# Later layers of a graph network: raw rows in places of their own that ScalarE frees, and more places for one-hots, cast halves and rows

## The chip, the cores and the metric

One Trainium2 chip; the program runs on one of its cores. The metric is the time of one execution on the device in microseconds (us), as the median of several runs. Engines are named TensorE (PE in the rows), VectorE (DVE), ScalarE (ACT), GpSimd (POOL) and SyncE (SP).

## The reference

x is 6250 nodes by 256 features; `src` and `dst` are the ends of 100000 edges, sorted by `dst`. Cut to what matters:

```python
xn = _layernorm(x)
h = xn
for layer in range(6):                        # _L0_gnn_ref
    agg = segment_sum(h[src], dst, num_segments=n)
    z = h + agg
    z = z @ W1[layer] + b1[layer]
    z = relu(_batchnorm(z, g1[layer], be1[layer]))
    z = z @ W2[layer] + b2[layer]
    z = _batchnorm(z, g2[layer], be2[layer])
    h = z if layer == 5 else relu(z)
x = x + h + _L0_mix_ref(xn)                   # attention-like mixing by heads of 32
x = x + _L0_ffn_ref(_layernorm(x))            # 8 experts, three 256x256 maps each
```

`_batchnorm` takes mean and variance over all nodes, so each of its twelve calls is a point at which everything waits for the last column.

## The kernel before, in words

The nodes are padded to 49 tiles of 128 (NT), in 7 chunks of 7 tiles (CT, NC). `Zt` holds the features transposed, two blocks of 128 (FB) by all nodes, in SBUF. The edges are 784 tiles of 128 in 7 sections (S) of 112. Of each section 62 tiles (AT) are summed densely: layer 0 builds a matrix of edge counts (`adjacency`, u8, in HBM), and a later layer multiplies it. The other 50 tiles (GS) are gathered row by row. A later layer has these parts:

- **Passage.** ScalarE applies the affine map and relu to a chunk, TensorE transposes it into banks 0 to 3 (`rows_of_h`), VectorE copies the rows into one of three row buffers `Rb` (`copy_rows`, L1543), and SyncE's queue stores them to `y_table` in HBM (`store_rows`, L575). Chunk c uses buffer c % 3, so a copy waits for the store of chunk c - 3. Then 8 warm-up matmuls (`warm`, L905).
- **Dense sums.** For a chunk's rows ScalarE writes the high terms (fp32r) into `Ych` (`high_terms`, L1274), VectorE the low terms, row minus high (`low_terms`, L1550). SyncE loads blocks of the adjacency into three `Land` places; ScalarE casts a block in two halves of 4 and 3 tiles (`cast_half`, L1300) into one of three places `Ac`, waiting for the half three back. TensorE multiplies a half (`dense_half`, L1021: 16 or 12 matmuls of 512 columns); after a block VectorE adds two banks into `Zt` (`add_dense`, L1682), and TensorE's block k waits for the adds of block k - 2. There are 98 halves: 6 come before the first quad, the others are spread over the first 74 quads by `halves_at`.
- **Quads.** 91 quads of up to 4 gathered tiles (N1). GpSimd issues an indirect DMA for each tile (`gather`, L755). The raw rows land in the low-term half of one of four quad places `Gsp` (RQ = 4), two in `G` and two in `BIG`, so the gather of quad n waits for the matmuls of quad n - 4. ScalarE writes the high terms (`quad_high`, L1282), then copies the raw rows to banks 6 and 7 (L1286), because the low terms overwrite them; VectorE writes the low terms from the banks (`quad_low`, L1558). VectorE makes a one-hot matrix for each tile (`one_hots`, L1568) in one of two places, for quad n + 1 as soon as quad n - 1 is done. TensorE multiplies (`quad`, L926); its last matmul signals `s_mmq`, which is also the signal for the dense halves of that step. Each group of three or four quads is summed over high and low terms (`group_rows`, L1655), transposed (L934) and added to `Zt` (`add_group`, L1668).
- **First map.** From quad 75 on (W1G) TensorE does parts of `z @ W1` between quads (`w1_part`, L1050), ScalarE evicts them (L1309), VectorE takes statistics (`z1_stats`: `part_stats`, L1686; `bank_stats`, L1692). Then `bn_coefficients` (aggregation at L1788), ScalarE's affine, and the second map (`w2_stage`, L1104) with statistics in the same manner.

The order on each engine is the order in which the functions write the steps: at step n VectorE does `quad_low(n)`, `one_hots(n + 1)`, the sum of a group that ended, the adds of the halves of step n - 1, the columns of a group, then statistics of step n - 2. Nothing is reordered on the chip, and a wait holds everything behind it on its engine. Layer 0 has GpSimd gather in another way (`raw0`) and takes its quads whole, in fp32; the part after layer 5 (mixing and experts) is not touched.

## Time and profile before

| | us |
|---|---|
| median of the 3 runs shown | 5272.77 |
| lowest, highest | 5271.77, 5281.3 |
| the profiled execution, its own time | 5229.82 |
| its span, first to last instruction | 5228.0 |
| layers 1 to 5, one each (end of the second map to end of the next) | 615.3 to 622.8 |
| the part after layer 5, from 4157 on | 1071 |

Busy times are those of the profiled execution, and an engine's busy time is no sign that it is the limit: what a place costs is read from what ends the idle time there. Start times in a timeline are us from the span's start. "issue" as a releaser means that the profile shows nothing that the engine waited for; "remote" means that the releaser is not among the instructions that were recorded.

### The profile page before, as it was taken

Reading aid. Unit: us, or ns where it says so; the run is one execution under the profiler, and the core shown is the slowest. Engines: PE = TensorE matmul, PEld = TensorE weight load, DVE = VectorE, ACT = ScalarE, POOL = GpSimd, SP = SyncE. Lnnn points to the kernel's source line nnn. Section 1 sums busy time; section 2 is a strip of 40 time slices with the busy share of each in tenths; the row PEclk is TensorE's granted clock in tenths of the full one; section 3 lists DMA queues with packets and bytes.
Section 4 is the critical chain, followed back from the end, with each engine's and each line's share of the span. In section 5 each row is a group of like instructions: output and inputs, shape, how many; then the busy total and the mean of one; then the engine's idle time right before and its main releaser. Section 6 shows DMA issues by size and latency. Waiting matters only on the chain.

```text
span 5228.0 us, 69828 instructions
## 1 busy us (share of the span) xinstructions
PE 4635.8 (89%) x19111; PEld 3326.3 (64%) x19111; DVE 3077.3 (59%) x7552; ACT 3090.9 (59%) x4248; POOL 2980.1 (57%) x3415
## 2 busy tenths in 40 slices
PE   4777899989887899888997998888898899999999
PEld 3555578667764677557775677646776576666665
DVE  6666666455555565545555455555555556666666
ACT  4555533367665676557675667656675435555555
POOL 5565566136662566626665266634666227877776
PEclk8999999999999999999998999989999989999999
DMA  6334454044432554334442354425443410000000
GB/s 208 109 123 130 132 165 144 27 158 152 143 117 68 160 155 145 102 105 145 151 137 85 119 154 152 128 57 166 149 146 114 150 37 8 8 8 8 8 8 8
DMA packets 197182, 560.41 MB, mean 107 GB/s; under 512 B 44306, under 2 KB 63228, under 8 KB 196668
## 3 DMA queue, kind: packets, MB, share of 16 engines
q0 software_dynamic: 109728, 299.78, 20.3%
q1 hardware_dynamic: 79676, 227.39, 12.2%
q10 hardware_dynamic: 7392, 28.90, 1.4%
q8 instruction: 144, 2.36, 0.2%
q14 instruction: 242, 1.98, 0.1%
HBM read 481.66 MB, written 74.24 MB: 106 GB/s over the span
## 4 chain that ended last, share of the span: by engine, by line
PE 54%; DVE 11%; another core or an unknown queue 11%; ACT 10%; issue 9%; POOL 3%; DMA 1%; DVEq 1%; ACTq 0%; POOLq 0%; SPq 0%
PE bank L1021 17%; PE bank L1204 10%; PE bank L1213 6%; PE bank L1104 5%; PE bank L926 4%; PE bank L923 3%; PE bank L969 3%; ACT bank L1286 3%; PE bank L1050 3%; ACT Gsp L1282 2%; ACT Ac L1300 2%; DVE Gsp L1558 2%; DVE onehot L1568 2%; DVE Z L1682 2%
## 5 line engine op out<-in xcount | busy, mean ns | idle before, releaser
L755 POOL DMA_INDIRECT G<-y_table,idx x1416 | 1376.6, 972 | 1335.4 <-DMA y_table<-BIG 512.2
L1021 PE MATMUL bank<-Ac,Ych 128*128 128x512 f32 x7644 | 1909.1, 402 | 166.7 <-issue 86.4
L1021 PEld LDWEIGHTS bank<-Ac,Ych 128*128 128x128 f32 x7644 | 1471.4, 194 | 544.7 <-issue 143.8
L1300 ACT CAST Ac<-BIG 128x2048 fp32r<-128x2048 uint8 (+1 forms) x546 | 916.4, 1688 | 735.7 <-remote 520.2
L755 POOL DMA_INDIRECT BIG<-y_table,idx x870 | 829.1, 953 | 492.2 <-issue 249.5
L1568 DVE TENSOR_SCALAR onehot<-iota,rel 128x128 fp32r<-128x128 f32 x2290 | 513.0, 298 | 696.0 <-remote 550.1
L1558 DVE TENSOR_TENSOR Gsp<-bank,Gsp 128x512 fp32r<-128x512 f32 x875 | 564.1, 685 | 362.6 <-ACT bank L1286 246.1
L2047 DVE TENSOR_TENSOR G<-G,bank 128x448 f32<-128x448 f32 x784 | 462.0, 619 | 215.4 <-ACT G L1464 114.2
L926 PE MATMUL bank<-Gsp,onehot 128*128 128x512 f32 x1750 | 518.7, 414 | 69.9 <-issue 34.2
L1682 DVE TENSOR_TENSOR Z<-Z,bank 128x512 f32 x546 | 373.8, 685 | 207.3 <-PE bank L1021 85.1
L1469 ACT ACTIVATE G<-G,fsh,fsc 128x448 f32<-128x448 f32 x448 | 333.9, 757 | 250.7 <-DVE G L2047 245.1
L1365 ACT CAST BIG<-bank 128x384 f32 (+2 forms) x672 | 276.8, 514 | 269.4 <-PE bank L969 148.1
L926 PEld LDWEIGHTS bank<-Gsp,onehot 128*128 128x128 f32 x1750 | 320.3, 190 | 172.3 <-issue 118.6
L969 PE MATMUL bank<-BIG 128*128 128x408 bf16 (+1 forms) x1302 | 292.6, 348 | 116.4 <-DVE BIG L1580 63.6
L1213 PE MATMUL bank<-BIG,G 128*128 128x256 f32 x1568 | 347.7, 379 | 2.3 <-ACT G L1469 2.3
L1050 PE MATMUL bank<-Z,W 128*128 128x448 f32 (+1 forms) x720 | 310.0, 582 | 39.7 <-ACT Z L1309 29.1
L1213 PEld LDWEIGHTS bank<-BIG,G 128*128 128x128 f32 x1568 | 297.8, 190 | 61.1 <-issue 20.4
L1686 DVE BATCH_NORM_STATS2 bst<-Z 128x6 f32<-128x448 f32 (+1 forms) x324 | 183.4, 608 | 184.9 <-ACT Z L1325 164.4
L923 PE MATMUL bank<-G,onehot 128*128 128x256 f32 x1072 | 276.8, 404 | 6.8 <-DMA G<-y_table,idx 4.1
L1286 ACT COPY bank<-G 128x512 f32<-128x512 f32 x440 | 243.3, 583 | 33.1 <-DVE Gsp L1558 31.7
L1104 PE MATMUL bank<-Z,W 128*128 128x448 f32 x672 | 254.2, 540 | 5.9 <-ACT Z L1256 5.9
L1050 PEld LDWEIGHTS bank<-Z,W 128*128 128x128 f32 x720 | 150.4, 217 | 168.2 <-issue 155.4
(229 smaller groups left out, 5785.5 us busy)
## 6 DMA issues: line engine op xcount, KB each, us to landing
BIG<-adjacency SPq DMA_DIRECT2D x273, 448.0 KB
BIG<-y_table SPq DMA_DIRECT2D x27, 896.0 KB
G<-y_table,idx POOLq DMA_INDIRECT x1416
y_table<-BIG SPq DMA_DIRECT2D x25, 896.0 KB, 3.8
adjacency<-BIG ACTq DMA_DIRECT2D x7, 3136.0 KB
BIG<-y_table,idx POOLq DMA_INDIRECT x870
BIG<-in_x SPq DMA_DIRECT2D x14, 896.0 KB, 7.4
y_table<-BIG ACTq DMA_DIRECT2D x7, 896.0 KB, 3.6
```

The source lines that it names most:

```text
L755: nc.gpsimd.indirect_dma_start(out=rows[:, j, :], out_offset=None, in_=y_table, in_offset=bass.IndirectOffsetOnAxis(ap=idx[:, t:t + 1], ax ...
L926: last = mm(group_bank(g)[:, 0:2 * D], onehot[:, q, j, :], Gsp[n % RQ][:, j, :, :].rearrange("p k f -> p (k f)"), start=start, stop=stop)
L1021: last = mm(bank[2 * (k % 2) + b][:, 0:UW], Ych[pos % 2][:, i, s, b * P:(b + 1) * P], Ac[x_ % NAC][:, i - CA * h, :], start=(i == 0 and s ...
L1050: last = mm(z1_bank(h, fo)[:, 0:n1 - n0], W1[:, b, fo * P:(fo + 1) * P], Zt[:, b, n0:n1], start=(b == 0), stop=(b == FB - 1))
L1104: last = mm(bank[2 * h + fo][:, 0:HN], W2[:, b, fo * P:(fo + 1) * P], Zt[:, b, n0:n1], start=(b == 0), stop=(b == FB - 1))
L1204: mm(product_bank(e, second, name)[:, 0:HN], w, x_, start=True, stop=True).then_inc(s_fh, 1)
L1213: last = mm(out_bank(e, k)[:, 0:D], h2T[:, b, k * P:(k + 1) * P], We[:, 2, e, b, :], start=(b == 0), stop=(b == FB - 1))
L1300: nc.scalar.copy(Ac[x_ % NAC][:, 0:t1 - t0, :], Land[k % NL][:, t0:t1, :]).then_inc(s_ac, 1)
L1558: last = tt(Gsp[n % RQ][:, j:j + 2, 1, :], quad_bank(j), Gsp[n % RQ][:, j:j + 2, 0, :].bitcast(fp32), ALU.subtract)
L1568: last = tsc(onehot[:, n % 2, j, :], iota[:, :], rel[:, t + j:t + j + 1], None, ALU.is_equal)
L1682: tt(win, win, bank[2 * (k % 2) + b][:, 0:UW], ALU.add).then_inc(s_dad, 1)
L2047: tt(to, a, product_bank(e, second, product_)[:, 0:HN], ALU.add).then_inc(s_fv, 1)
```

## The change

In layers 1 to 5 the raw rows of a quad get places of their own: three of 4 KB a partition in `BIG`. There are three `Gsp` places instead of four. A gather waits for ScalarE's copies of the quad three back (`s_gh`) instead of TensorE's matmuls of the quad four back. For the last quad of a layer (N1 - 1) ScalarE makes no copy to a bank, and VectorE takes the low terms from the raw rows in SBUF. The one-hots have three places (OH), in layer 0 too. Later layers have a fourth place for a cast half, `Acx` (three tiles, always an odd half), in the row buffer of the first chunk in order; to leave that free, later layers load rows into two buffers in turn, and a load waits for the low terms of the chunk two back. In the passage chunk 3 has a fourth row place `Rx` with a semaphore of its own, `s_yx`, so chunk 6 waits for the store of chunk 0, not 3. The low terms of the first chunk in order are split: GpSimd does tiles 0 to 3 (`first_low_terms`, signal `s_slp`), VectorE tiles 4 to 6. The aggregation of a feature block stands right behind its last statistics, and one set of statistics at the end of the stage stands behind the last quad's low terms.

The diff, cut:

```diff
-    RQ, RQ0 = 4, 4
+    RQ, RQ0, OH = 3, 4, 3
...
-    NAC = 3
+    NAC, NACL = 3, 4
...
-              for i, a in enumerate((AC_AT, AC_AT + AC_BYTES, 2 * QUAD_BYTES))]
+              for i, a in enumerate((AC_AT, AC_AT + AC_BYTES, QUAD_BYTES + RQ * RAW_BYTES))]
...
+        Acx = f32r_at("Acx", [P, CT - CA, UW], BIG_AT + RB_AT + (NC - NRB) % NRB * RB_BYTES)
+        Rx = at(0, RB_BYTES).rearrange("p (t f) -> p t f", f=D)
...
-        raw = [places[q // 2].rearrange("p (q j k f) -> p q j k f", q=2, j=GJ, k=2)[:, q % 2, :, 1, :] for q in range(RQ)]
+        raw = [at(QUAD_BYTES + q * RAW_BYTES, RAW_BYTES).rearrange("p (j f) -> p j f", j=GJ) for q in range(RQ)]
...
-        def row_buffer(pos):
-            return CHUNKS[pos % NRB] % NRB
+        def row_buffer(pos, l=0):
+
+            if first_layer(l) or pos < NRB:
+                return CHUNKS[pos % NRB] % NRB
+            return CHUNKS[1 + (pos - 1) % 2] % NRB
...
+        def cast_place(l, x_):
+
+            return Acx if x_ % casts(l) == NAC else Ac[x_ % casts(l)]
...
             def gather(l, n):
...
-                turn = RQ0 if first_layer(l) else RQ
-                if n >= turn:
-                    hold(pool, s_mmq, quads_before(l) + n - turn + 1)
+                if first_layer(l):
+                    if n >= RQ0:
+                        hold(pool, s_mmq, n - RQ0 + 1)
+                elif n >= RQ:
+                    hold(pool, s_gh, (l - 1) * N1 + n - RQ + 1)
...
+            def first_low_terms(l):
+
+                hold(pool, s_sh, l * NC + 1)
+                nc.gpsimd.tensor_tensor(Ych[0][:, 0:CA, 1, :], Rb[row_buffer(0)][:, 0:CA, :],
+                                        Ych[0][:, 0:CA, 0, :].bitcast(fp32), ALU.subtract).then_inc(s_slp, 1)
...
             def quad_high(l, n):
...
-                nc.scalar.copy(Gsp[n % RQ][:, 0:tiles(n), 0, :], rows[:, 0:tiles(n), :])
+                last = nc.scalar.copy(Gsp[n % RQ][:, 0:tiles(n), 0, :], rows[:, 0:tiles(n), :])
+                if n == N1 - 1:
+                    last.then_inc(s_gh, 1)
+                    return
...
             def cast_half(l, x_):
...
-                if x_ >= NAC:
-                    act.wait_ge(*dense_done(l, x_ - NAC))
+                if x_ >= casts(l):
+                    act.wait_ge(*dense_done(l, x_ - casts(l)))
+                elif x_ == NAC:
+
+                    act.wait_ge(s_yd[row_buffer(0)], stored(l, CHUNKS[0]))
+                    act.wait_ge(s_slp, l)
+                    act.wait_ge(s_sl, l * NC + 1)
...
             def one_hots(l, n):
...
-                if n >= 2:
-                    dve.wait_ge(s_mmq, quads_before(l) + n - 1)
+                if n >= OH:
+                    dve.wait_ge(s_mmq, quads_before(l) + n - OH + 1)
...
             def bank_stats(k, h, n, there, value, l, second):
...
                     V.bn_stats(bst[:, b, k, :], z1_bank(h, b)[:, 0:n]).then_inc(s_bst, 1)
+                    hold(dve, s_bst, (l * (W1_PARTS + HALVES) + W1_PARTS + second * HALVES - 1) * FB + b + 1)
+                    V.bn_aggr(bmv[:, b, :], bst[:, b, 0:parts, :].rearrange("p a s -> p (a s)")).then_inc(s_bn, 1)
...
-                    if n > 1 and w1_at(l, n - 2) is not None:
-                        z1_stats(l, w1_at(l, n - 2))
+                    for m in () if n in (0, 1, N1 - 2) else (n - 3, n - 2) if n == N1 - 1 else (n - 2,):
+                        if w1_at(l, m) is not None:
+                            z1_stats(l, w1_at(l, m))
```

The order on GpSimd at the start of a later layer's gathers, before (with the semaphores that a row waits for; `s_yd` are stores, `s_mmq` TensorE's quads):

```order
L324 ISA [waits s_yd1,s_yd2]
L755 DMA G<-y_table,idx 128x256 [waits s_yd0]
L755 DMA G<-y_table,idx 128x256 x7
L755 DMA BIG<-y_table,idx 128x256 x8
L324 ISA
L755 DMA G<-y_table,idx 128x256 [waits s_mmq]
L755 DMA G<-y_table,idx 128x256 x3
L324 REGISTER_ALU
L755 DMA G<-y_table,idx 128x256 [waits s_mmq]
```

And now (`s_sh` is ScalarE's high terms, `s_gh` its copies of a quad; the subtraction stands ahead of the check for stray edges, some rows above the gathers):

```order
L825 TENSOR_TENSOR Ych_49<-BIG,Ych_49 128x4x256 [waits s_sh]
L795 TENSOR_LOAD flag
L795 ISA x2
L796 COMPARE_AND_BRANCH
L326 ISA
```

and, from the wait for the stores on:

```order
L326 ISA [waits s_yd1,s_yd2]
L326 REGISTER_ALU [waits s_yd0]
L778 DMA BIG<-y_table,idx 128x256 [waits s_yx]
L778 DMA BIG<-y_table,idx 128x256 x11
L326 ISA
L778 DMA BIG<-y_table,idx 128x256 [waits s_gh]
L778 DMA BIG<-y_table,idx 128x256 x3
L326 REGISTER_ALU
L778 DMA BIG<-y_table,idx 128x256 [waits s_gh]
```

The subtraction has come ahead, and each further quad waits for ScalarE instead of TensorE.

The order on ScalarE from the first halves of layer 1 on, before (`s_dn` and `s_mmq` are TensorE's, `s_ap` landed blocks, `s_g` landed rows, `s_gl` VectorE's low terms; `Ac` and `Gsp` have numbers of the allocator):

```order
L1300 CAST Ac_53<-BIG 128x1536 [waits s_dn]
L1300 CAST Ac_51<-BIG 128x2048 [waits s_dn,s_ap0]
L1282 CAST Gsp_54<-G 128x4x256 [waits s_g0]
L1286 COPY bank<-G 128x512 x2
L1300 CAST Ac_52<-BIG 128x1536 [waits s_dn]
L1282 CAST Gsp_55<-G 128x4x256 [waits s_g1]
L1286 COPY bank<-G 128x512 [waits s_gl]
L1286 COPY bank<-G 128x512
L1300 CAST Ac_53<-BIG 128x2048 [waits s_dn,s_ap1]
L1282 CAST Gsp_56<-BIG 128x4x256 [waits s_g2]
```

And now:

```order
L1343 CAST Acx<-BIG 128x1536 [waits s_sl,s_slp,s_yd1]
L1309 CAST Ych_50<-BIG 128x7x256 [waits s_rc]
L1343 CAST Ac_51<-BIG 128x2048 [waits s_dn,s_ap2]
L1343 CAST Ac_52<-BIG 128x1536 [waits s_dn]
L1343 CAST Ac_53<-BIG 128x2048 [waits s_dn,s_ap0]
L1317 CAST Gsp_55<-BIG 128x4x256 [waits s_g0]
L1324 COPY bank<-BIG 128x512 x2
L1343 CAST Acx<-BIG 128x1536 [waits s_dn]
L1317 CAST Gsp_56<-BIG 128x4x256 [waits s_g1]
L1324 COPY bank<-BIG 128x512 [waits s_gl]
```

The fourth half of the layer has gone ahead of its wait for TensorE, into `Acx`, and each later one waits one half further back.

The order on VectorE at the last quad of layer 1, before:

```order
L1558 TENSOR_TENSOR Gsp_55<-bank,Gsp_55 128x2x256 x2
L1568 TENSOR_SCALAR onehot<-iota,rel 128x128 x2
L1686 BN_STATS bst<-Z 128x6 x2
L1558 TENSOR_TENSOR Gsp_56<-bank,Gsp_56 128x2x256
L1655 TENSOR_REDUCE G<-bank 128x256
```

And now:

```order
L1603 TENSOR_TENSOR Gsp_57<-bank,Gsp_57 128x2x256 x2
L1613 TENSOR_SCALAR onehot<-iota,rel 128x128 x2
L1603 TENSOR_TENSOR Gsp_55<-BIG,Gsp_55 128x2x256
L1731 BN_STATS bst<-Z 128x6 x2
L1700 TENSOR_REDUCE G<-bank 128x256
```

The statistics of 426 columns stood ahead of the last low terms and now stand behind them; the low terms read `BIG`, not a bank. Behind these, at the last statistics, before and now:

```order
L1568 TENSOR_SCALAR onehot<-iota,rel 128x128 x4
L1686 BN_STATS bst<-Z 128x6 x2
L1692 BN_STATS bst<-bank 128x6 x2
L1788 BN_AGGR bmv<-bst 128x2 x2
L1790 TENSOR_TENSOR bmu<-bmv,parl 128x2
```

```order
L1613 TENSOR_SCALAR onehot<-iota,rel 128x128 x4
L1731 BN_STATS bst<-Z 128x6 x2
L1738 BN_STATS bst<-bank 128x6
L1740 BN_AGGR bmv<-bst 128x2
L1738 BN_STATS bst<-bank 128x6
L1740 BN_AGGR bmv<-bst 128x2
L1836 TENSOR_TENSOR bmu<-bmv,parl 128x2
```

The first aggregation has come between the statistics of the two feature blocks.

## Rows read from the trace of the kernel before

**Rows 1.** The page: busy time of each engine, share of the span, instructions

```profile
PE 4635.8 (89%) x19111; PEld 3326.3 (64%) x19111; DVE 3077.3 (59%) x7552; ACT 3090.9 (59%) x4248; POOL 2980.1 (57%) x3415
```

**Rows 2.** Windows of layer 2: length; busy PE, PEld, DVE, ACT, POOL; clock; DMA

```profile
1740.00:2150.00 410.00, 370.93 (x1566) 294.31 (x1566) 236.46 (x584) 292.17 (x306) 259.98 (x273) 0.97 0.47 144
2150.00:2260.00 110.00, 85.75 (x261) 50.96 (x262) 62.87 (x162) 49.84 (x88) 58.27 (x62) 0.88 0.27 78
```

**Rows 3.** TensorE's waits in layers 1 to 5: total us, times, longest

```profile
PE bank L1021 <- issue: 82.1, 116, 2.4
PE bank L1021 <- DVE Z L1682: 74.2, 36, 5.2
PE bank L934 <- DVE G L1655: 54.0, 15, 7.2
PE bank L926 <- issue: 34.2, 42, 3.0
PE bank L926 <- DVE Gsp L1558: 34.0, 29, 3.9
```

**Rows 4.** Timeline of layer 2, one late signal: start, us, engine, line

```profile
2047.77 0.87 DVE L1568 TENSOR_SCALAR onehot<-iota,rel 128x128 fp32r<-128x128 f32 x4 [6.39 <-remote]
2047.82 1.90 ACT L1300 CAST Ac<-BIG 128x2048 fp32r<-128x2048 uint8 x1 [7.76 <-remote]
2048.51 0.94 POOL L755 DMA_INDIRECT G<-y_table,idx  x1 [2.96 <-remote]
2048.62 1.52 DVE L1682 TENSOR_TENSOR Z<-Z,bank 128x512 f32 x2
...
2050.20 1.22 PE L1021 MATMUL bank<-Ac,Ych 128*128 128x512 f32 x2 [4.23 <-DVE Z L1682]
```

**Rows 5.** Timeline of the passage to layer 2

```profile
1702.22 1.67 ACT L1274 CAST Ych<-BIG 128x1792 fp32r<-128x1792 f32 x1
1702.86 4.34 DVE L1543 COPY BIG<-bank 128x512 f32<-128x512 f32 x8 [1.24 <-DMA y_table<-BIG]
...
1705.51 3.62 PE L905 MATMUL bank<-ones 128*128 128x256 f32 x16
1707.11 2.43 DVE L1550 TENSOR_TENSOR Ych<-BIG,Ych 128x256 fp32r<-128x256 f32 x7
...
1709.60 0.73 PE L1021 MATMUL bank<-Ac,Ych 128*128 128x512 f32 x2 [0.47 <-DVE Ych L1550]
```

**Rows 6.** Groups of GpSimd in the last part of the program: busy, mean ns

```profile
L816 POOL TENSOR_TENSOR BIG<-G 128x448 f32<-128x448 f32 x56 | 64.0, 1143 | 51.3 <-ACT G L1469 51.2
...
L810 POOL TENSOR_TENSOR W<-W,BIG 128x128 f32<-128x128 f32 x112 | 51.7, 462 | 0.0
```

**Rows 7.** Timeline of VectorE at the end of layer 1

```profile
1682.64 0.61 DVE L1692 BATCH_NORM_STATS2 bst<-bank 128x6 f32<-128x426 f32 x1 [0.35 <-PE bank L1104]
...
1683.75 1.21 DVE L1788 BATCH_NORM_AGGREGATE bmv<-bst 128x2 f32<-128x84 f32 x2 [0.50 <-DVE bst L1692]
```

**Rows 8.** Timeline of layer 2's last quad

```profile
2247.56 0.59 ACT L1286 COPY bank<-BIG 128x512 f32<-128x512 f32 x1 [0.81 <-DVE Gsp L1558]
...
2247.84 1.10 DVE L1686 BATCH_NORM_STATS2 bst<-Z 128x6 f32<-128x426 f32 x2
...
2248.85 0.67 DVE L1558 TENSOR_TENSOR Gsp<-bank,Gsp 128x512 fp32r<-128x512 f32 x1
...
2250.41 0.69 DVE L1655 TENSOR_REDUCE G<-bank 128x256 f32<-128x512 f32 x1 [0.88 <-PE bank L926]
```

**Rows 9.** Timeline of layer 2: quad 3 on TensorE, the copies of quad 4

```profile
1752.19 1.07 PE L926 MATMUL bank<-Gsp,onehot 128*128 128x512 f32 x4
...
1754.52 1.10 ACT L1286 COPY bank<-G 128x512 f32<-128x512 f32 x2
```

**Rows 10.** ScalarE's waits for landed rows, layers 1 to 5

```profile
ACT Gsp L1282 <- DMA BIG<-y_table,idx: 29.5, 19, 3.1
...
ACT Gsp L1282 <- DMA G<-y_table,idx: 19.3, 11, 3.0
```

More of the change, by code:

```diff
@@ L407, in loaded, with casts @@
                 return (first.index(pos) + 1) * LANES
-            later = [p for p in first if p >= NRB]
+            later = [p for p in range(NRB, NC) if row_buffer(p, l) == i]
             return (len(first) + (l - 1) * len(later) + later.index(pos) + 1) * LANES
+        def casts(l):
+            return NAC if first_layer(l) else NACL
+        def cast_place(l, x_):
+            return Acx if x_ % casts(l) == NAC else Ac[x_ % casts(l)]
         def gathered(l, n):
@@ L1536, in copy_rows @@
             def copy_rows(l, c):
-                if c >= NRB:
-                    dve.wait_ge(s_yd[c % NRB], stored(l, c - NRB))
+                before = max((k for k in range(c) if k != NRB and k % NRB == c % NRB), default=None)
+                if c != NRB and before is not None:
+                    dve.wait_ge(s_yd[c % NRB], stored(l, before))
                 for m in range(YP):
@@ L1548, in low_terms @@
                 dve.wait_ge(s_sh, l * NC + pos + 1)
[L1549 to L1550 removed]
+                for i in range(0 if first_layer(l) or pos > 0 else CA, CT):
+                    last = tt(Ych[pos % 2][:, i, 1, :], Rb[row_buffer(pos, l)][:, i, :],
                               Ych[pos % 2][:, i, 0, :].bitcast(fp32), ALU.subtract)
@@ L1783, in bn_coefficients @@
             def bn_coefficients(l, second):
-                n, o, parts = 2 * l + second, 3 * second, (W1_PARTS, HALVES)[second]
-                hold(dve, s_bst, (l * (W1_PARTS + HALVES) + W1_PARTS + second * HALVES) * FB)
-                step = steps(s_bn, n * N_BN, N_BN)
-                for b in range(FB):
-                    step(V.bn_aggr(bmv[:, b, :], bst[:, b, 0:parts, :].rearrange("p a s -> p (a s)")))
+                n, o = 2 * l + second, 3 * second
+                hold(dve, s_bn, n * N_BN + FB)
+                step = steps(s_bn, n * N_BN + FB, N_BN - FB)
                 step(tt(bmu[:, :], bmv[:, :, 0], parl[:, o, :], ALU.add))
```

71 lines of the change are left out of this document (42 added, 29 removed).

## Prediction

> **What bounds the kernel now.** I read the page first: of a span of 5228.0 us TensorE is busy 89%, the other four engines 59% and less [rows 1]. The change touches layers 1 to 5 alone, apart from the third one-hot place and the order of the normalisation, which layer 0 has too. So the next view is the windows: the dense and gather stage of layer 2 takes 410 us with TensorE busy for 370.9, GpSimd for 260 (the rows count 0.95 of each 1.25 us that a row's gather needs), VectorE for 236 and ScalarE for 292; then 110 us follow, with the first linear map, with TensorE busy for 85.8 [rows 2]. TensorE bounds the stage, but it is idle for 12% of the two windows together, and its granted clock falls from 2.4 to 1.2 GHz for parts of both (means of 0.97 and 0.88).
>
> What ends that idle time is in TensorE's waits over the five layers [rows 3]. 82.1 us before dense matmuls have no releaser at all: the stream pauses by itself, and no buffer can mend that. 74.2 us in 36 waits end with the adds of dense sums (L1682), 34.0 us in 29 waits with the low terms of a quad (L1558) and 54.0 us in 15 waits with the sum of a group (L1655). The timeline shows what such a wait is made of [rows 4]: at 2047.8 VectorE, ScalarE and GpSimd all start within 0.8 us, since TensorE's signal comes late, after one of its own pauses. VectorE then makes four one-hots first (0.87 us, from 2047.77), then two adds (1.52 us, from 2048.62), and only then does TensorE go on, at 2050.20. The one-hots hold up the adds only because, with two places, both wait for the same signal.
>
> **The change part by part.**
>
> Third one-hot place. One-hots of quad n+1 wait for quad n-2 instead of n-1, so VectorE makes them before the late signal comes and then starts with the adds or with the group's sum. Each of TensorE's waits behind L1682 or L1655 shrinks by up to 0.87 us. There are 36 + 15; five of the 15 are the last group of a layer, without one-hots ahead, which leaves 46. I opened the waits of layer 2 in the timeline: one-hots stand right ahead of the adds in all seven behind L1682, but once VectorE came to them late from a quad's low terms and not from a signal, and that one gives nothing. I take 38 of the 46 for that: 38 x 0.87 = **33 us**. Bounds: 0 (something else is then last) and 46 x 0.87 = 40. Behind the one-hots on VectorE nothing else moves.
>
> Fourth cast place, three raw places freed by ScalarE, three quad places. Casts wait for the half four back, and the GpSimd queue no longer waits for TensorE but for ScalarE's two copies of the quad three back. TensorE waited for a cast only rarely, so this works through ScalarE: it gets to the quads earlier, and some of the 34.0 us before L926 go. In the opposite direction, four places for quads become three, and ScalarE's cast of quad n waits for quad n-3; TensorE needs it two steps after, so that costs nothing as long as ScalarE is not later than that. I take **5 us**, one wait of 1 us in each layer, near the low end, because in layer 2 the longest of these waits stands behind a chunk's low terms on VectorE, which stay. Bounds: a gain of 34 + 43 (what is left of the 74.2 without the 36 x 0.87), and a loss, for which see the rivals.
>
> The first chunk's low terms. Now VectorE copies rows until 1707.2 (1707.11 is the first subtraction) and then subtracts seven tiles, 2.43 us, until 1709.54; TensorE's first dense matmul is at 1709.60, but its warm-up matmuls run until 1709.13 [rows 5]. GpSimd is to do four tiles from the end of ScalarE's 1.67 us cast at 1703.89. Its subtractions of 128 and 448 elements took 462 and 1143 ns [rows 6], 2.1 ns an element, so 1024 elements take about 0.19 + 2.17 = 2.4 us: done at 1706.3. Then the warm-up sets the start: 0.47 us a layer, **2.5 us** in all (the five layers differ little). The other three tiles on VectorE (1.1 us) are needed 3.6 us later. The stores of rows keep their order and their pace, so the table is complete as late as before, and the first gather too. The row place for chunk 3 removes a wait that this trace hardly has: VectorE's wait of 1.24 us in rows 5 is for the store of chunk 2, and that one stays. So: nothing. GpSimd did nothing before its gathers, whose cover ends with the table at about 1712, so 2.4 us of work lie hidden there. Both bounds of this part: 2.5 gained, or 2.4 us lost in each passage, 12 us, if the subtraction holds up VectorE's copies, which no row of before shows side by side. I take the gain: in the last part of the program, beside VectorE's work, GpSimd's four groups of 128 elements differ by 4 ns in the mean, the longest being the one in rows 6, so nothing there speaks of one holding up the other. The Trainium skill ("SBUF — State Buffer", Who interferes with whom) has VectorE and GpSimd sharing one port pair as an exclusive lock, but frees an instruction of VectorE with at most one SBUF input outside the two-port modes. By that rule the copies go on and the 2.5 stand; read without the exception it would be a loss of 12, and the sum 33 instead of 47.
>
> Aggregation between the two last statistics. After the second linear map VectorE has a statistic of block 0, waits 0.35 us for TensorE, does block 1, waits again 0.50 and aggregates both in 1.21 us [rows 7]. The first aggregation (0.55) now fills the first gap. Block 1's statistic starts some 0.3 later at most, so 0.6 us are left, six times (layers 0 to 5): **3.5 us**. After the first map TensorE is not waited for there: nothing.
>
> The last quad of a layer. Its low terms come at 2248.85 because ScalarE copies to the bank first (0.59 us after a wait of 0.81) and VectorE has statistics of 1.10 us ahead of them [rows 8]. Without the copy and with the statistics behind, they start near 2247.9. The statistics then end at about 2249.7, a little after the quad's matmuls, so the group's sum starts there instead of at 2250.41: 0.7 us, five times, **3.5 us**. What is late next is VectorE with those statistics.
>
> Sum: 33 + 5 + 2.5 + 3.5 + 3.5 = 47.5, taken as 47. The profiled execution took 5229.8 us (span 5228.0 and 1.8 around it); it would take 5183. The runs shown have a median of 5272.77, 43 above the profiled one, which I can't explain from the trace; I take the gain off the median: **5226 us**.
>
> **Rivals.**
>
> All waits behind VectorE go. With ScalarE and GpSimd a step further ahead, the 43 us left behind L1682 and the 34.0 before L926 vanish too. For it: ScalarE waited for the signal at nearly every cast, as at 2047.8 [rows 4]. Against: VectorE's order still puts low terms and adds in one queue. Time: 5273 - 47 - 43 - 34 + 5 = 5154. The granted clock pulls the same way: a mean of 0.88 in the second window [rows 2] means a quarter of it at 1.2 GHz, and each idle stretch fewer can give some of it back. The Trainium skill ("TensorE: Matmul & The Clock Gate", HAM oscillation — how this bites in real kernels) says that pauses between bursts make the clock fall each time, with half of the throttled time lost; by it the gain would be above the sum of the waits, and the trace agrees in so far as such windows have low clocks.
>
> The time comes back. TensorE's pauses with no releaser (82.1 and 34.2 us, [rows 3]) are not in any buffer's reach; if what is saved in a wait is lost in the next pause, or VectorE's next instruction is late instead, only the serial parts remain: 2.5 + 3.5 + 3.5 = 9.5, 5263 us, inside what a measurement of this kernel can tell from no change (0.2%, 10.5 us).
>
> Slower: the rows come late. GpSimd's next quad now waits for ScalarE's copies. In layer 2 quad 3's matmuls end at 1753.26, while the copies of quad 4 end at 1755.62 [rows 9], and it is on these that the gather of quad 7 would now wait: 2.4 us later than before. ScalarE already waited for landed rows 30 times (19 + 11, 48.8 us in all [rows 10]). If the fourth cast place brings ScalarE no nearer, each of these 30 grows by 2.4: 72 us against the 47, so 5273 + 25 = 5298. The point from which it decides: when the copies of quad n-3 end more than the slack between landing and ScalarE's cast after quad n-4. Against it: both sides now buffer three quads, six where there were four, and ScalarE's wait reaches one half further back.
>
> **How the numbers follow.** Forecast 0.58 (5200 to 5250), all waits go 0.16 (5154 to 5200), the time comes back 0.15 (5252 to 5265), slower 0.11 (5283 and more). Faster by over 0.2%: 0.58 + 0.16 = 0.74; same 0.15; slower 0.11. The range from 5160 to 5265 leaves out the slower case and the end of the best one.
>
> **What would show it.** In the new trace the one-hots should no longer stand between a late signal and the adds, and the waits of L1021 behind the adds should fall from 74.2 to some 45 us. The first dense matmul should follow the warm-up within 0.1 us, with GpSimd's subtraction near 2.4 us and VectorE's copies unchanged. GpSimd's waits should name ScalarE instead of TensorE. The forecast is wrong if the pauses without releaser grow by as much as the waits fall, or if ScalarE's waits for landed rows pass 100 us.

## The result, and the profile after

The changed kernel took 5592.67 us, the median of 4 runs (5591.74 to 5611.81), and the kernel before beside it 5272.27 (4 runs). The ratio is 1.0615, with an interval of 1.0587 to 1.0643: slower by 6%, 320 us, where I had forecast 47 us less.

A session here is a group of runs made together on one chip. The pair above comes from one in which TensorE's stream pauses with no releaser in the profile, as in the rows ahead of the prediction; in most later sessions the very same kernel before took 4674 us, with next to no such pauses. I call the two conditions "with pauses" and "without pauses", and the time of every experiment is compared with the kernel before of its own session. The two traces of this section are 364 us apart and not 320, since the profiled execution of the kernel before took 5230 us.

The page of the changed kernel, engines' busy time, with pauses, answers to [rows 1]:

```profile
PE 4782.2 (86%) x19111; PEld 3402.9 (61%) x19111; DVE 3060.7 (55%) x7532; ACT 3092.5 (55%) x4243; POOL 2987.0 (53%) x3420
```

The gather stage of layer 2, from the first quad to 10 us after the last, in two windows, answers to [rows 2] (columns: length, busy and count of each engine, granted clock, DMA share, GB/s):

```profile
1815.00:2290.00 475.00, 397.31 (x1531) 305.91 (x1532) 228.25 (x570) 286.19 (x299) 259.12 (x273) 0.88 0.41 124
2290.00:2413.00 123.00, 91.40 (x298) 57.37 (x297) 69.08 (x175) 56.62 (x92) 58.65 (x62) 0.89 0.24 70
```

The stage takes 598 us where it took 520, and the clock is 0.88 where the first window had 0.97. From first to last quad the five layers together take 2917 us where they took 2560, so the loss lies here. GpSimd's work is as long as before, 259 + 59 us against 260 + 58: it does not gather more slowly, it stands still for longer. The groups of the gathers, the dense matmuls and the quads over layers 1 to 5 answer to [rows 3] (columns: line, engine, operation, tiles, shape and count; busy us and mean ns; idle us before them and what ended it):

```profile
L778 POOL DMA_INDIRECT BIG<-y_table,idx x1750 | 1664.7, 951 | 1362.2 <-ACT bank L1324 817.8 <-issue 544.5
L1056 PE MATMUL bank<-Ac,Ych 128*128 128x512 f32 x5420 | 1448.3, 415 | 255.4 <-issue 209.0 <-DVE Z L1727 40.6
...
L957 PE MATMUL bank<-Gsp,onehot 128*128 128x512 f32 x1750 | 548.3, 431 | 108.5 <-issue 58.7 <-DVE Gsp L1603 48.9
...
L1056 PE MATMUL bank<-Acx,Ych 128*128 128x512 f32 x1440 | 406.6, 426 | 62.2 <-issue 60.4
```

The waits behind the adds (now L1727) fell from 74.2 to 40.6 us, as forecast. But the waits without releaser before dense matmuls and quads grew from 82.1 + 34.2 to 209.0 + 60.4 + 58.7 us, by 212; the busy time of the same matmuls grew by 172 (1712.4 + 518.7 to 1448.3 + 406.6 + 548.3), with a matmul at 415 to 431 ns where it took 402 and 414. Together that is 384 us, against 364 between the two traces. And GpSimd, which I had thought freer, waits 817.8 us for ScalarE.

The timeline shows one such pause. GpSimd's queue from 1453 on, layer 1 of the changed kernel (columns: start, length, engine, line, operation, idle time before):

```profile
1453.24 0.95 POOL L778 DMA_INDIRECT BIG<-y_table,idx  x1 [2.96 <-ACT bank L1324]
1454.50 0.94 POOL L778 DMA_INDIRECT BIG<-y_table,idx  x1 [0.30 <-issue]
...
1470.78 0.95 POOL L778 DMA_INDIRECT BIG<-y_table,idx  x1 [0.30 <-issue]
1472.03 0.95 POOL L778 DMA_INDIRECT BIG<-y_table,idx  x1 [0.30 <-issue]
1480.72 0.94 POOL L778 DMA_INDIRECT BIG<-y_table,idx  x1 [7.74 <-ACT bank L1324]
```

Sixteen gathers in a row, 1.25 us apart, from 1453.24 to 1473. TensorE in the same stretch:

```profile
1464.49 2.88 PE L1056 MATMUL bank<-Ac,Ych 128*128 128x512 f32 x12
1467.21 0.61 PE L957 MATMUL bank<-Gsp,onehot 128*128 128x512 f32 x2
1467.67 0.39 PE L1056 MATMUL bank<-Ac,Ych 128*128 128x512 f32 x1
1470.31 0.39 PE L1056 MATMUL bank<-Ac,Ych 128*128 128x512 f32 x1 [2.25 <-issue]
1471.71 0.58 PE L1056 MATMUL bank<-Ac,Ych 128*128 128x512 f32 x1 [1.02 <-issue]
1473.80 5.77 PE L1056 MATMUL bank<-Ac,Ych 128*128 128x512 f32 x13 [1.50 <-issue]
```

At 1467.7, 14.4 us after the run of gathers began, its stream comes down to one matmul at 1467.67, one at 1470.31, one at 1471.71; at 1473.80, 0.8 us after the last gather of the run, it goes on. VectorE, ScalarE and then GpSimd wait for it meanwhile (8.65, 8.61 and 7.74 us before their next instructions at 1476.01, 1476.07 and 1480.72). The granted clock falls too: it is 1.00 from 1450 to 1467.7, 0.50 (1.2 GHz) from 1473.80 to 1475.90 and 1.00 again from 1479 on, and the matmul at 1471.71 takes 0.58 us where the two before it take 0.39: so the busy time grows with the pauses. I laid all the pauses (over 0.5 us with no releaser) of both traces beside the runs of gathers (less than 1.45 us apart): in the changed kernel the median pause begins 14.7 us after its run began and ends 1.3 us after the run ended; before, 14.6 and 1.2 us. What differs is the runs in layers 1 to 5: 62 of exactly 12 gathers and 19 longer ones before, 29 of 12 and 69 longer ones after, 55 of them of 16. The waits over 0.5 us without a releaser that fall into runs of more than 12 gathers come to 39 us before and 246 after, those in runs of 12 or fewer to 72 and 82. The 15 us are a median and no threshold: in the kernel before a quarter of the pauses begin less than 6 us after their run began. Even the late signal of [rows 4] is of this kind; GpSimd's queue in the kernel before:

```profile
2030.65 0.95 POOL L755 DMA_INDIRECT BIG<-y_table,idx  x1 [2.49 <-PE bank L926]
2031.90 1.06 POOL L755 DMA_INDIRECT BIG<-y_table,idx  x1 [0.30 <-issue]
...
2044.60 0.95 POOL L755 DMA_INDIRECT G<-y_table,idx  x1 [0.30 <-issue]
2048.51 0.94 POOL L755 DMA_INDIRECT G<-y_table,idx  x1 [2.96 <-remote]
```

Twelve gathers end at 2045.5; with the limit at TensorE's quad four back, the run stops at about the moment when the pause begins (15 us), and the pause is short. With ScalarE's copies as the limit a run goes on to 16, 20 us, and the pause goes on with it.

### The profile page after: what moved, and what is told of

It reads as the page before. It is cut to its first block, busy times and chain, and to the rows that moved or that the text cites. A ratio compares the mean times of both kernels' runs of the same rounds, so it can differ in the third digit from the quotient of the medians.

```text
span 5591.7 us, 69863 instructions
## 1 busy us (share of the span) xinstructions
PE 4782.2 (86%) x19111; PEld 3402.9 (61%) x19111; DVE 3060.7 (55%) x7532; ACT 3092.5 (55%) x4243; POOL 2987.0 (53%) x3420
## 3 DMA queue, kind: packets, MB, share of 16 engines
q0 software_dynamic: 109728, 299.78, 18.8%
## 4 chain that ended last, share of the span: by engine, by line
PE 64%; another core or an unknown queue 11%; issue 9%; DVE 9%; ACT 5%; DMA 1%; POOL 1%; DVEq 1%; ACTq 0%; POOLq 0%; SPq 0%
PE bank L1056 26%; PE bank L1239 10%; PE bank L957 6%; PE bank L1248 5%; PE bank L1139 4%; PE bank L954 3%; PE bank L1085 3%; PE bank L1000 3%; DVE Gsp L1603 1%; DVE Z L1727 1%; DVE onehot L1613 1%; ACT Z L1291 1%; DVE BIG L1625 1%; ACT bank L1324 1%
## 5 line engine op out<-in xcount | busy, mean ns | idle before, releaser
L778 POOL DMA_INDIRECT BIG<-y_table,idx x1750 | 1664.7, 951 | 1362.2 <-ACT bank L1324 817.8
L1056 PE MATMUL bank<-Ac,Ych 128*128 128x512 f32 x6204 | 1647.8, 414 | 261.0 <-issue 214.4
L1056 PEld LDWEIGHTS bank<-Ac,Ych 128*128 128x128 f32 x6204 | 1233.8, 200 | 611.2 <-issue 310.5
L1343 ACT CAST Ac<-BIG 128x2048 fp32r<-128x2048 uint8 (+1 forms) x426 | 738.8, 1747 | 716.2 <-remote 543.8
L1727 DVE TENSOR_TENSOR Z<-Z,bank 128x512 f32 x546 | 375.3, 687 | 792.7 <-remote 491.8
L778 POOL DMA_INDIRECT G<-y_table,idx x536 | 536.3, 1000 | 349.1 <-issue 158.1
L957 PE MATMUL bank<-Gsp,onehot 128*128 128x512 f32 x1750 | 548.3, 431 | 108.5 <-issue 58.7
L1324 ACT COPY bank<-BIG 128x512 f32<-128x512 f32 x870 | 481.9, 585 | 204.2 <-DVE Gsp L1603 185.8
L1613 DVE TENSOR_SCALAR onehot<-iota,rel 128x128 fp32r<-128x128 f32 x2290 | 511.7, 297 | 128.4 <-remote 114.3
L1317 ACT CAST Gsp<-BIG 128x1024 fp32r<-128x1024 f32 (+1 forms) x455 | 460.7, 1013 | 75.3 <-remote 61.2
L1056 PE MATMUL bank<-Acx,Ych 128*128 128x512 f32 x1440 | 406.6, 426 | 62.2 <-issue 60.4
L1056 PEld LDWEIGHTS bank<-Acx,Ych 128*128 128x128 f32 x1440 | 300.2, 210 | 152.0 <-issue 88.4
L1085 PE MATMUL bank<-Z,W 128*128 128x448 f32 (+1 forms) x720 | 298.6, 564 | 60.4 <-ACT Z L1352 45.6
L1700 DVE TENSOR_REDUCE G<-bank 128x256 f32<-128x512 f32 x140 | 96.3, 688 | 406.5 <-remote 355.9
```

The lines of the kernel that those rows point to most:

```text
L778: nc.gpsimd.indirect_dma_start(out=rows[:, j, :], out_offset=None, in_=y_table, in_offset=bass.IndirectOffsetOnAxis(ap=idx[:, t:t + 1], ax ...
L957: last = mm(group_bank(g)[:, 0:2 * D], onehot[:, q, j, :], Gsp[n % RQ][:, j, :, :].rearrange("p k f -> p (k f)"), start=start, stop=stop)
L1056: last = mm(bank[2 * (k % 2) + b][:, 0:UW], Ych[pos % 2][:, i, s, b * P:(b + 1) * P], cast_place(l, x_)[:, i - CA * h, :], start=(i == 0 a ...
L1085: last = mm(z1_bank(h, fo)[:, 0:n1 - n0], W1[:, b, fo * P:(fo + 1) * P], Zt[:, b, n0:n1], start=(b == 0), stop=(b == FB - 1))
L1324: last = nc.scalar.copy(quad_bank(j), rows[:, j:j + 2, :])
L1343: nc.scalar.copy(cast_place(l, x_)[:, 0:t1 - t0, :], Land[k % NL][:, t0:t1, :]).then_inc(s_ac, 1)
```

## The experiments

**Parts undone (without pauses).** The expectations of these four were written for the condition with pauses, and their session was of the other kind: the kernel before took 4673.85 us. The edits are cut; e4 also has the place `filler`, its semaphore and a first memset ahead of the layers.

```diff
 # e1: in gather(l, n), after the wait for s_gh
+                    if n > RQ:
+                        hold(pool, s_mmq, quads_before(l) + n - RQ)
 # e2
-    RQ, RQ0, OH = 3, 4, 3
+    RQ, RQ0, OH = 3, 4, 2
 # e3
-    NAC, NACL = 3, 4
+    NAC, NACL = 3, 3
 # e4: in gather(l, n)
+                    if n % 3 == 0:
+                        for f in range(3):
+                            hold(pool, s_fill, 1 + ((l - 1) * 30 + n // 3 - 1) * 3 + f)
+                            nc.gpsimd.memset(filler[:, :], 0.0).then_inc(s_fill, 1)
```

> The changed kernel with GpSimd's old wait added to the new one: a quad's gather waits for ScalarE's copies of the quad three back and for TensorE's matmuls of the quad four back. Theory A (long runs of gathers): in the changed kernel GpSimd issues 16 to 20 gathers in a row, and some 15 us after such a run began TensorE's stream goes down to one instruction in 0.7 or 1.4 us until the run ends; with runs of 12 at most the time falls to 5210 to 5290 us and TensorE's waits without releaser at the dense matmuls of layers 1 to 4 from 269 us to under 110. Theory B (the third one-hot place or the fourth cast place does it): the time stays within 5550 to 5600. Theory C (GpSimd freed by ScalarE is later, rows come late): no change either, or slower still.

> The changed kernel with two one-hot places instead of three. Theory A (long runs of gathers): 5560 to 5640 us, since the runs stay; at most the 33 us of my prediction are lost. Theory B (the third place does it): under 5400.

> The changed kernel with three cast places in every layer instead of four in layers 1 to 5. Theory A (long runs of gathers): 5540 to 5610 us; the runs may be a little shorter, since ScalarE is held a half sooner. Theory B (the fourth place, another address or ScalarE further ahead, does it): under 5400.

> The changed kernel with a break on GpSimd's queue ahead of every third quad: three memsets of 384 elements, each waiting for the one before, an estimate of 1 to 2.5 us from the 462 ns of a subtraction of 128 elements and the 1143 ns of one of 448. No wait for TensorE comes back. Theory A (a run's length without a break counts): TensorE's stalls get rarer, and the time falls by 100 us and more, below 5480. Theory A2 (the mean rate of gathers counts, or a backlog that such a break does not clear): the stalls stay, 5560 to 5620. Theory C (the rows come late): the added work makes it slower, 5610 to 5700.

Measured: e1 4658.4 (ratio 0.9965, 0.9952 to 0.9977), e2 4640.81 (0.9934, 0.9917 to 0.9950), e3 4660.99 (0.9973, 0.9962 to 0.9984), e4 4857.83 (1.0398, 1.0380 to 1.0415). So they decide nothing on the pauses, and what e4 was made for, whether a break within a run ends them, stays untested. What e4 says is something else. Its row of memsets:

```profile
L781 POOL MEMSET filler<- 128x384 f32 x450 | 192.8, 429 | 46.1 <-POOL filler L781 46.0
```

450 memsets put 193 + 46 = 239 us on GpSimd's queue, and the kernel takes 218 us more than the changed one: without pauses GpSimd's queue sets the length of the stage.

**Both kernels as they are (without pauses).**

> The changed kernel as it is, since in the runs of the experiments the kernel before took 4674 us where it had taken 5272, and TensorE's waits without releaser at the dense matmuls were under 1 us in all. Theory D (the pauses of TensorE's stream without releaser are a condition of the chip or of the moment, and the loss of the change is their growth alone): where the kernel before takes about 4674, the changed one is faster than it, 4625 to 4665; where the kernel before takes about 5270, it is slower, about 5590. Rival E (the change is slower by something of its own, whatever the pauses): slower than the kernel before in both, by 1% and more.

> The kernel before as it is, for its trace in the same condition. Theory D: where it takes about 4674, the dense matmuls have under 5 us of waits without releaser in layers 1 to 4 (82 us in the trace of the prediction), and GpSimd has idle time only behind TensorE; its ratio to itself is 1.

Measured: the changed kernel 4639.68, the kernel before 4673.39; ratio 0.9928 (0.9914 to 0.9941). Theory D holds for this half, rival E falls: here the change is 34 us faster. The kernel before against itself gave 1.0000 (0.9990 to 1.0009). The five layers in the kernel before, without pauses:

```profile
L1021 PE MATMUL bank<-Ac,Ych 128*128 128x512 f32 x6860 | 1618.3, 390 | 2.7 <-DVE Ych L1550 2.7
...
L755 POOL DMA_INDIRECT G<-y_table,idx x880 | 837.8, 952 | 812.0 <-DMA y_table<-BIG 500.7 <-issue 254.2 <-PE bank L926 57.2
L755 POOL DMA_INDIRECT BIG<-y_table,idx x870 | 826.8, 950 | 266.2 <-issue 247.3 <-PE bank L926 18.9
...
L926 PE MATMUL bank<-Gsp,onehot 128*128 128x512 f32 x1750 | 497.7, 406 | 33.2 <-DVE Gsp L1558 33.2
```

and in the changed kernel:

```profile
L778 POOL DMA_INDIRECT BIG<-y_table,idx x1750 | 1665.8, 952 | 575.2 <-issue 518.1 <-ACT bank L1324 57.0
L1056 PE MATMUL bank<-Ac,Ych 128*128 128x512 f32 x5420 | 1279.9, 389 | 0.1
...
L957 PE MATMUL bank<-Gsp,onehot 128*128 128x512 f32 x1750 | 502.4, 408 | 20.5 <-DVE Gsp L1603 20.4
...
L1056 PE MATMUL bank<-Acx,Ych 128*128 128x512 f32 x1440 | 346.5, 389 | 0.0
```

The 82.1 us without releaser are gone in the kernel before too, and so are the 74.2 us behind the adds: those waits came with the pauses. The windows of layer 2, from the first quad to the last and to the next layer's first quad, before and then changed:

```profile
1506.10:1941.30 435.20, 422.23 (x1793) 331.42 (x1794) 293.43 (x726) 338.53 (x385) 317.60 (x334) 0.99 0.51 154
1941.30:2041.60 100.30, 91.29 (x374) 61.30 (x372) 49.13 (x107) 64.47 (x81) 15.45 (x16) 1.00 0.34 122
```
```profile
1497.00:1925.70 428.70, 419.85 (x1793) 331.75 (x1794) 294.20 (x725) 339.82 (x384) 317.81 (x334) 0.99 0.52 157
1925.70:2024.50 98.80, 91.16 (x373) 61.19 (x372) 48.19 (x103) 64.51 (x81) 17.57 (x17) 1.00 0.35 123
```

From first to last quad 435.2 us become 428.7, and the passage 98.8 instead of 100.3. GpSimd needs 350 x 1.25 = 438 us of its queue for a layer's gathers, the first of which start some 21 us ahead of the first quad (in layer 2 from 1484.1 to 1933.8, 450 us, before, and from 1475.6 to 1918.8, 443 us, in the changed kernel), and its idle time behind TensorE or ScalarE fell from 57.2 + 18.9 = 76 to 57 us in five layers. Does a transfer take longer in one condition? The gathers' own queue on the page (packets, MB, share of 16 engines), with pauses and without:

```profile
q0 software_dynamic: 109728, 299.78, 18.8%
```
```profile
q0 software_dynamic: 109728, 299.78, 22.1%
```

18.8% of 5591.7 and 22.1% of 4637.9 are 1051 and 1025 us: the time of the packets differs by under 3%, where the two executions differ by 20%.

**The serial parts alone, and a tighter limit (without pauses).** e8 is the kernel before with the first chunk's low terms on GpSimd, the aggregation between the statistics and the last quad without a copy. e5 is the changed kernel with this:

```diff
                     hold(pool, s_gh, (l - 1) * N1 + n - RQ + 1)
+                    hold(pool, s_mmq, quads_before(l) + n - RQ + 1)
```

> The changed kernel in which a quad's gather also waits for TensorE's matmuls of the quad three back, so that runs of gathers are cut shorter than in the kernel before. Theory D (two conditions): where the kernel before takes about 4674, TensorE's stream has no pauses without releaser, GpSimd's 350 gathers of 1.25 us set the stage, and every wait added to its queue costs: 4670 to 4760 (the gate at four back took 4658, the changed kernel 4640). Where the kernel before takes about 5272, shorter runs cut the pauses: 5150 to 5300, far below the 5592 of the changed kernel. Rival: GpSimd's queue has room, 4640 to 4655.

> The kernel before with the serial parts of the change alone: the first chunk's low terms on GpSimd, the aggregation between the last statistics, the last quad without a copy. My prediction's terms for them are 2.5 + 3.5 + 3.5 = 9.5 us; in the traces of the old and the changed kernel side by side the stretch from the last quad's end to the next layer's first quad is 101.2 against 100.0 us, so here I expect 4662 to 4672. Rival (GpSimd's gathers start later behind its subtraction, or the last statistics are now late): 4674 or more.

Measured: e5 4774.65 (1.0211, 1.0194 to 1.0228), e8 4667.46 (0.9989, 0.9979 to 0.9999), so 6 us for the serial parts, by the interval between 0.5 and 10.

**Neither the wait nor the place (with pauses).** e10 is the changed kernel with e1's wait and e3's three cast places together. In its session the kernel before took 5234.65 us.

> The changed kernel with three cast places in every layer and with GpSimd's wait for TensorE's matmuls of the quad four back: both halves of what lets GpSimd and ScalarE run ahead undone. With the cast place alone undone it took 4661, with the wait alone back 4658, with neither undone 4640. If the two only work together (the gathers run on only where ScalarE, which frees their places, is itself not held by TensorE): 4658 to 4665 here, where the kernel before takes about 4674. If they add up (21 + 19): about 4680. Where the kernel before takes about 5272: theory D has the pauses bounded by runs of 12 again, 5210 to 5290, against 5592.

Measured: 5229.19 us, ratio 0.9991 (0.9980 to 1.0001). Its runs of more than 12 gathers are 12, where the kernel before has 19 and the changed one 69. The whole loss is gone with these two parts undone, though the third one-hot place, the serial parts and the row places are all still there. Its rows:

```profile
L1058 PE MATMUL bank<-Ac,Ych 128*128 128x512 f32 x6860 | 1711.7, 402 | 159.6 <-issue 83.1 <-ACT Ac L1345 58.3 <-DVE Z L1729 16.6
L780 POOL DMA_INDIRECT BIG<-y_table,idx x1750 | 1664.0, 951 | 1009.4 <-issue 508.8 <-remote 281.8 <-PE bank L959 189.2
...
L959 PE MATMUL bank<-Gsp,onehot 128*128 128x512 f32 x1750 | 521.5, 416 | 76.0 <-DVE Gsp L1605 47.2 <-issue 27.3
```

The waits without releaser are back at 83.1 + 27.3. Note the second and third name in the first row: the waits behind the adds fell from 74.2 to 16.6 us, and 58.3 us behind ScalarE's casts stand in their place.

**More sessions.** Which of the two parts makes the loss was open, and only a session with pauses can show it. e11 to e13 repeat e1, e3 and e5, e14 repeats e1, e17 and e19 repeat e5, and e15 and e18 are the changed kernel with the wait at the quad five back:

```diff
                     hold(pool, s_gh, (l - 1) * N1 + n - RQ + 1)
+                    if n > RQ + 1:
+                        hold(pool, s_mmq, quads_before(l) + n - RQ - 1)
```

> GpSimd's old wait added to the changed kernel, as in e1, in another session. If the kernel before takes about 4674 again, 4658 again. If it takes about 5235 to 5272: theory A/D (a pause of TensorE begins some 15 us after a run of gathers begins and ends when the run ends, so what counts is how long a run may get) expects 5190 to 5250; the fourth cast place then costs nothing. Rival B (ScalarE further ahead by the fourth cast place makes the pauses longer): 5350 to 5600.

> The changed kernel with three cast places, as in e3. Where the kernel before takes about 4674, 4661 again. Where it takes 5235 to 5272: theory A/D expects that the runs of gathers still get longer than 12, since ScalarE's copies free them, so 5350 to 5600; rival B expects a return to about 5230.

> The changed kernel with gathers held to TensorE's matmuls of the quad three back, as in e5. Where the kernel before takes about 4674, 4775 again. Where it takes 5235 to 5272: runs are cut below 12, so the pauses without releaser almost go (under 30 us in layers 1 to 5 at the dense matmuls), and what is left is the cost that it has in the other condition: 4850 to 5100. If the mean rate of gathers and not the length of a run makes the pauses: 5250 and more.

> The changed kernel with GpSimd's old wait for the matmuls of the quad four back added (as e1), once more for a session in which the kernel before takes 5235 to 5272. There theory A/D (a pause begins some 15 us after a run of gathers begins and ends when the run ends; the length of a run is what counts) expects 5190 to 5250 in spite of the fourth cast place. Rival B (the fourth cast place makes the pauses longer) expects 5350 to 5600. Where the kernel before takes 4674: 4658.

> The changed kernel with GpSimd's wait for the matmuls of the quad five back added. With it at three back it took 4775, at four back 4658, without it (ScalarE's places alone bind, in effect six back) 4640, where the kernel before takes 4674. There I expect 4640 to 4650. Where the kernel before takes 5235 to 5272, theory A/D (a run of gathers gets one quad of four longer than before, so each of some 17 pauses a layer may last up to 5 us longer) expects 5330 to 5530, between 5229 and 5592; rival B (the fourth cast place, the wait makes no difference) expects 5550 and more.

> The changed kernel with gathers held to TensorE's matmuls of the quad three back, alone in its session. Where the kernel before takes 4674: 4775. Where it takes 5235 to 5272: runs stay below 12 gathers, so TensorE's pauses without releaser almost go at the dense matmuls of layers 1 to 5 (83 us with the wait at four back), and the time is near what it is in the other condition: 4850 to 5100. If any gathering and not the length of a run makes the pauses: 5250 and more.

> The changed kernel with GpSimd's wait for the matmuls of the quad five back, in another session. Where the kernel before takes 4674: 4642. Where it takes 5235 to 5272: theory A/D expects 5330 to 5530, since a run may get 16 gathers where 12 were allowed, and only the slack beyond that is cut. If only runs beyond 16 hurt: 5230 to 5280.

> The changed kernel with gathers held to TensorE's matmuls of the quad three back, as in e17. Where the kernel before takes 4674: 4775. Where it takes 5235 to 5272: 4850 to 5100, with TensorE's pauses without releaser at the dense matmuls under 30 us in layers 1 to 5; if any gathering makes the pauses: 5250 and more.

All of these fell into sessions without pauses (kernel before 4672 to 4676): e11 4657.57, e12 4663.85, e13 4774.6, e14 4656.32, e15 4641.78 (0.9931, 0.9912 to 0.9951), e18 4641.92, e17 4776.23, e19 4781.89. They repeat to within 0.2% what their first runs gave and add one thing: with the limit at five quads back nothing is lost against the changed kernel (4641.8 against 4639.7), at four back 18 us, at three back 135.

**The wait alone off (with pauses).** e16 is e3 once more, and its session had pauses (kernel before 5270.12 us).

> The changed kernel with three cast places (as e3), for a session in which the kernel before takes 5235 to 5272 us. There theory A/D expects 5400 to 5600, since the wait is still off GpSimd's queue and the runs get longer than 12; rival B (the fourth cast place) expects 5220 to 5260. Where the kernel before takes 4674: 4661.

Measured: 5573.19 us, ratio 1.0573 (1.0527 to 1.0619). Its rows:

```profile
L1056 PE MATMUL bank<-Ac,Ych 128*128 128x512 f32 x6860 | 1832.1, 416 | 293.8 <-issue 242.5 <-ACT Ac L1343 29.8 <-DVE Z L1727 13.9
L778 POOL DMA_INDIRECT BIG<-y_table,idx x1750 | 1660.8, 949 | 1339.2 <-ACT bank L1324 794.4 <-issue 544.9
...
L957 PE MATMUL bank<-Gsp,onehot 128*128 128x512 f32 x1750 | 544.4, 432 | 101.0 <-DVE Gsp L1603 68.9 <-issue 31.1
```

e10 and e16 differ in one thing, GpSimd's wait for TensorE's quad four back: with it 5229 against 5235, without it 5573 against 5270. The runs of more than 12 gathers go from 12 to 53, and the waits without releaser from 110 to 274 us. GpSimd's idle time beside its own issue was 501 us, behind TensorE's signals, and is 794, behind ScalarE, though it may run further ahead. So of the 320 us some 303 come with the loss of that wait; rival B, the fourth cast place, falls, and what is left for it is the difference between 1.0573 and 1.0615, whose intervals overlap. e16 rests on two runs, in another session than e10, but 5.8% is far above what sessions with pauses differ by (5235 and 5270).

Two things were never met with pauses. The wait put back with the fourth cast place kept (e1, e11, e14) would show whether it alone mends the changed kernel. The limit at three quads back (e5, e13, e17, e19) and the break of e4 would tell the length of a run from the mean rate of gathers, or from a backlog that builds up over several runs. That the length of a run is what counts is therefore argued, from the timelines and from the counts of runs in e10 and e16, and not shown by an edit that changes it alone.

## Why the prediction was wrong

**The step that failed** is in the part on the fourth cast place and the raw places freed by ScalarE: 5 us gained, bounded by "a gain of 34 + 43" and "a loss, for which see the rivals". It measured 303 us lost, with pauses (e16 against e10 and the kernel before). I counted the removed wait as freedom for GpSimd. In that condition it was a brake that stopped most runs of gathers at 12 or fewer, at about the time when TensorE's pause begins. The reading under it failed too: 82.1 us "have no releaser at all: the stream pauses by itself, and no buffer can mend that". The pauses do not stand by themselves. In the median they begin 14.6 us after a run of gathers begins and end 1.2 us after it ends, and that could be read from the trace of before, by laying GpSimd's timeline beside TensorE's. I never asked what the other engines did at the start of a pause, only at its end.

**The rivals.** The slower one had the right edit and the wrong price: rows that come late by 2.4 us, 30 times, 5298. The rows were not late: ScalarE waited for landed rows for 48.8 us before and for 0.6 us, once, in the changed kernel. "The time comes back" was the nearest, but I let it end at 5263, as if what is saved could at most be lost again. A pause whose length hangs on how far the others may run ahead has no such limit. My sign of a wrong forecast, that the pauses grow by as much as the waits fall, did come: the one fell by 34, the other grew by 212.

**Third one-hot place, 33 us.** The rows moved as I said: 74.2 to 40.6 here, to 16.6 in e10. The time did not. In e10 the same waits end with ScalarE's casts, 58.3 us, and the whole of that kernel gains 5 us, about what the serial parts give, with an interval that reaches no change. Without pauses the waits behind the adds are zero to begin with, and the third place is worth 1 us by the medians (e2, 4640.81 against 4639.68), which is inside the noise. After a late signal all engines start together, and by these rows taking 0.87 us off the one that is last brings up the next.

**First chunk's low terms, 2.5 us.** Right in its mechanism (though five times 0.47 is 2.4). Layer 2 of the changed kernel, with pauses:

```profile
1775.50 6.50 DVE L1587 COPY BIG<-bank 128x512 f32<-128x512 f32 x12 [0.71 <-DMA y_table<-BIG]
1779.63 2.37 POOL L825 TENSOR_TENSOR Ych<-BIG,Ych 128x1024 fp32r<-128x1024 f32 x1 [87.28 <-ACT Ych L1309]
1780.32 3.62 PE L936 MATMUL bank<-ones 128*128 128x256 f32 x16
1783.58 0.58 PE L1056 MATMUL bank<-Ac,Ych 128*128 128x512 f32 x1
```

GpSimd's subtraction takes 2.37 us (2.4 forecast), the dense matmuls follow the warm-up at once, and VectorE's 12 copies take 6.50 us in one piece up to 1782.0, 0.54 us each as in [rows 5] (8 in 4.34), so the subtraction beside them did not hold them up. On the port that VectorE and GpSimd share (the Trainium skill, "SBUF — State Buffer", Who interferes with whom) the rule with its exception agrees with this row.

**Last quad, 3.5 us, and the aggregation, 3.5 us.** In the changed kernel without pauses the last two tiles' low terms follow right behind the one-hots:

```profile
1922.24 1.29 DVE L1603 TENSOR_TENSOR Gsp<-bank,Gsp 128x512 fp32r<-128x512 f32 x2 [1.37 <-ACT bank L1324]
1923.44 0.47 DVE L1613 TENSOR_SCALAR onehot<-iota,rel 128x128 fp32r<-128x128 f32 x2
1923.83 0.68 DVE L1603 TENSOR_TENSOR Gsp<-BIG,Gsp 128x512 fp32r<-128x512 f32 x1
1924.43 1.10 DVE L1731 BATCH_NORM_STATS2 bst<-Z 128x6 f32<-128x426 f32 x2
1925.76 0.69 DVE L1700 TENSOR_REDUCE G<-bank 128x256 f32<-128x512 f32 x1 [0.23 <-PE bank L957]
1927.09 0.42 DVE L1713 TENSOR_TENSOR Z<-Z,bank 128x256 f32 x1 [0.63 <-PE bank L965]
1927.42 0.67 DVE L1613 TENSOR_SCALAR onehot<-iota,rel 128x128 fp32r<-128x128 f32 x3
```

From the end of these one-hots (L1613, 1923.91) to the group's sum (1925.76) it takes 1.85 us; in the kernel before, without pauses, the same stretch is 1938.86 to 1941.36, 2.50 us. That is 0.65 a layer where I had 0.7. Together with the other serial parts e8 measured 6.1 us for the 9.5 of the sum; I did not take the three apart.

**The clock.** That it would add to a gain was a remark beside the rival; it added to the loss: 0.950 before, 0.912 after, and 0.98 in the runs without pauses. The Trainium skill ("TensorE: Matmul & The Clock Gate", HAM oscillation — how this bites in real kernels) says that pauses between bursts make the clock fall each time, and the trace agrees in kind: the clock is 0.50 right after the pause shown above, and the dense matmuls' and quads' busy time is 172 us longer. Its half of the throttled time was not tested here.

**Without pauses** the forecast of 47 us stands against 34 measured, but from other places: 6 from the serial parts, 1 from the one-hots, and the other 27 from the part that I had at 5. Neither half of that part gives much alone: with the cast place alone undone the kernel takes 4661, with the wait alone back 4658, where 4667 is the kernel with the serial parts only. My reading is that GpSimd can run on only where ScalarE, which frees its places, is itself not held by TensorE; the run with both undone, which would test it, met a session with pauses.

## What to carry to other kernels

When a trace has idle time without a releaser, lay the timelines of all engines side by side at its start and at its end before calling it the engine's own: here a queue on another engine set both ends. A wait that looks like mere back-pressure may also limit a burst, so when it is taken away, ask how long that engine may now run without a break, and keep a looser limit: five quads back kept the whole gain without pauses, though what it does with pauses was not met. And time a change in more than one session: the same edit was 6% slower in one and 0.7% faster in the other.

## What was not expected of the hardware

The same program took 5272, 5235 and 5270 us in some sessions and 4672 to 4676 in the others, steady within 0.5% in each. The 43 us between the profiled execution and the median, which the prediction could not explain, are about what the sessions with pauses differ by. Which condition a session meets does not hang on the chip alone: of the runs that the record gives to chip 9, e6 and e7 had no pauses and e10 had them, and of those on chip 7, e16 had them and e19 had none. The difference lies where GpSimd gathers: from the last quad of layer 5 to the end the kernel before took 1121 us with pauses and 1122 without. In a session with pauses TensorE's stream comes down to one instruction in 0.7 or 1.4 us, in the median after some 15 us of gathers at 1.25 us each, until they stop: two starts of its matmuls and weight loads lie 0.65 to 0.75 us apart 520 times in layers 1 to 5 of the changed kernel, 250 times in the kernel before and 43 times in the kernel before without pauses. In a session without, GpSimd gathers on for hundreds of us beside a TensorE that is hardly ever interrupted (0.1 us of idle time before its 5420 dense matmuls in the rows of the changed kernel above). What differs between the sessions, and what it is that the gathers take from TensorE, stays open: the packets' time is within 3%, and no row shows it. Whether a limit tighter than that of the kernel before would beat it in a session with pauses is open too (e17 was made for it), since no run of it met one.
